# Involution on one core: one tap moves from VectorE to GpSimd, its weight copies go to ScalarE, and some steps change their tick

## The chip, the cores and the metric

The kernel runs on 1 core of one Trainium2 chip. The metric is the device time of one execution in microseconds (us). The core has five engines that work side by side and meet at semaphores: TensorE (PE in the profile), VectorE (DVE), ScalarE (ACT), GpSimd (POOL) and SyncE (SP, which issues most transfers). SBUF is the working memory, PSUM (eight banks, the tensor `ps`) the memory that TensorE writes and GpSimd doesn't reach.

## The reference

Layer 0 is an involution with a residual, layer 1 attention and a routed feed-forward block. Only layer 0 is touched. For each pixel it computes 49 weights (7 x 7 taps) per channel group, takes a softmax over them, and sums 49 shifted, weighted copies of the image:

```python
def _L0_conv_ref(x, ...):            # x: 4 x 256 x 56 x 56, group-normalized
    x1, x2, x3 = conv1x1(x, w1, b1), conv1x1(x, w2, b2), conv1x1(x, w3, b3)   # 32, 32 and 256 channels
    p = conv1x1(position(h, w, x.dtype), wp, bp)
    sub2 = x1[:, :, None] - unfold_patches(x2)      # 49 taps, reflect padding 3
    subp = p[:, :, None] - unfold_patches(p)
    y = relu(bn_eval(concatenate([sub2, subp]), ...))
    y = relu(bn_eval(conv1x1(y, cw1), ...))
    wgt = softmax(conv1x1(y, cw2, cb2), axis=2)     # over the 49 taps
    out = 0
    for idx in range(49):                           # i, j = idx // 7, idx % 7
        patch = x3p[:, :, i:i + h, j:j + w].reshape(n, 32, 8, h, w)
        out = out + patch * wgt[:, :, idx][:, :, None]
    return out
```

## The kernel before

**Bands.** After a first stage of projections the image is worked off in 14 bands of 4 rows (`RW`, `NW`); the 128 partitions hold 4 images x 32 groups. Two bands are always under way: band `b` is summed, while the weights of the next one, `a`, are computed. One such step is a `slot(a, b)`; each engine has its own `slot`, and a loop runs six times over two slots, with one slot before it and one behind it (`slots`). The slot of the last band has no `a`.

**Ticks.** A slot has 20 ticks (`NPAIR_D`), counted by `u`. The order of the work on each engine is written out by hand: lists say at which tick a step is issued, and every engine takes its instructions in that order.

**Summing band b.** Taps 0 to 38 (`ND`) are VectorE's, two at a time, nineteen pairs and a twentieth with one tap; taps 39 to 48 (`OWN`, ten) are GpSimd's. For a pair `p`, ScalarE copies the weights to a PSUM bank (`weights`, L519) and once more beside the products, as the ninth row that becomes the denominator (`denominators`, L526). VectorE multiplies the 8 channels of the window by them (`pair`, L689) into one of two buffers. TensorE adds the buffer to four PSUM banks with an identity matrix (`add`, L847). For one of its taps, GpSimd multiplies (L319) and copies the weights beside it (L320), into one of two buffers `own_buf`; TensorE adds it, ticks 10 to 19 (`OWN_AT`). When all 49 are added (`acc_done`), VectorE takes the reciprocal of the denominator (L638) and multiplies (L642), `divide`, and TensorE may begin the next band. Row `i` of the exponentials holds taps 7i to 7i + 6; a tap waits for its row (`exped`).

**The weights of band a.** GpSimd subtracts, `z(a, i)` (L287), for each of seven tap rows. ScalarE applies a ReLU (`first`, L532, at ticks 0, 1, 3, 5, 7, 9, 11). Then a chain of 14 steps, one a tick from tick 1 (`CH_AT`): TensorE (L818, L823), ScalarE (`second`, L543), TensorE (L834), ScalarE (`third`, L550, which writes the logits `lg`). All use the same PSUM banks, so the next begins when the last is written. `z(a, 5)` waits for the matmuls of tick 8, `z(a, 6)` for those of tick 10. VectorE takes a running maximum over tap rows (`rowmax`, L655; `MAX_AT`: rows 1 and 2 ahead of pair 9, the others ahead of pairs 11, 13, 15, 17) and then folds it to one value per pixel (L662 to L670, `maxed`). GpSimd subtracts that from the logits row by row (`shift`, L298), row 0 after all but two of its taps and row 1 after them; ScalarE takes the exponential (`expo`, L506), row 0 at tick 18, rows 1 to 6 in the next slot at ticks 0, 2, 4, 6, 8, 10 (`EXP_NEXT`). GpSimd's whole order is `POOL_ORDER`.

Of the kernel before, what the change touches and what calls it, by code (L numbers as in the profile page):

```python
# [15 lines left out]
P = 128  # L16
# [11 lines left out]
RW = 4  # L28
# [16 lines left out]
OWN = 10  # L45
ND = TAPS - OWN
NPAIR_D = (ND + 1) // 2
NCH = 2 * K7
# [6 lines left out]
MAX_AT = [CH_AT[2 * max(i, 2) + 1] + 3 for i in range(K7)]  # L55
FOLD_AT = MAX_AT[-1]
EXP_NOW_AT = FOLD_AT + 1
EXP_NEXT = {0: 1, 2: 2, 4: 3, 6: 4, 8: 5, 10: 6}
# [3 lines left out]
OWN_AT = [NPAIR_D - OWN + k for k in range(OWN)]  # L62
# [60 lines left out]
def conv_stage(nc, planes, x2_dram, a1_dram, pf_dram, cw1_bd, cw2_bd, ident_dram, conv_dram, keep):  # L123
    ctx = ExitStack()
    with ctx:
# [150 lines left out]
        def _(pool):  # L276
# [12 lines left out]
            def shift(b, i):  # L289
                pool.wait_ge(maxed, b.n + 1)  # L290
                if not b.early(1):
                    pool.wait_ge(den_in, NPAIR_D * (b.n - 1) + FREE_ROW_PAIRS if i < FREE_ROW else NPAIR_D * b.n)
                if i == FREE_ROW and not b.early(1):
                    pool.wait_ge(own_ready, 2 * OWN * b.n)
                if b.early(1) and i in (1, 4):
                    pool.wait_ge(planes_out[i % 2], 16 * NSTORE[i % 2])
                m = mx[:].rearrange("p (h w) -> p h w", w=W).unsqueeze(2).broadcast_to([P, RW, K7, W])
                pool.tensor_tensor(ex[:, i], lg[:, i], m, ALU.subtract).then_inc(shifted, 1)  # L298

            def own(b, k):  # L300
                t = ND + k
                i, j = t // K7, t % K7
                if k == 0:
                    pool.wait_ge(win_in[b.par], 16 * (b.half + 1))
                    if b.early(1):
                        pool.wait_ge(proj_done, NUNIT)
                if k == 1 and b.early(1):
                    pool.wait_ge(a1_out, 16 * NBK)
                pool.wait_ge(exped, b.q(i) + 1)
                if k == 0 and not b.early(1):  # L310
                    pool.wait_ge(acc_done, b.n)
                if k == 1 and not b.early(1):
                    pool.wait_ge(stored, 16 * RW * b.n)
                if k >= 2:
                    pool.wait_ge(own_used, (OWN - 1) * b.n + k - 1)
                w = ex[:, i, :, j, :]
                xw = win[b.par][:, i:i + RW, 0:SHARE, j:j + W]
                o = own_buf[k % 2]
                pool.tensor_tensor(o[:, :, 0:SHARE], w.unsqueeze(2).broadcast_to([P, RW, SHARE, W]), xw, ALU.mult).then_inc(own_ready, 1)  # L319
                pool.tensor_copy(o[:, :, SHARE], w).then_inc(own_ready, 1)  # L320
# [182 lines left out]
        def _(act):  # L503
# [10 lines left out]
            def weights(b, p):  # L514
                n = min(2, ND - 2 * p)
                act.wait_ge(exped, b.q((2 * p + n - 1) // K7) + 1)
                if not (b.early(1) and p < 2):
                    act.wait_ge(prod_ready, NPAIR_D * b.n + p - 1)
                act.activation(ps[:, 2 + p % 2, 0:n * PW].rearrange("p (n h w) -> p n h w", h=RW, w=W), tap_pair(p),  # L519
                               ACT.Copy).then_inc(w_out, 1)  # L520

            def denominators(b, p):
# [3 lines left out]
                act.activation(prod[p % 2][:, 0:n, :, SHARE], tap_pair(p), ACT.Copy).then_inc(den_in, 1)  # L526
# [28 lines left out]
            def slot(a, b):  # L555
                first, second, third = chain(a, b)
                for u in range(NPAIR_D if b else 0):
# [4 lines left out]
                    if a and b and u == EXP_NOW_AT:  # L562
                        expo(a, 0)
                    if b and u + 1 < NPAIR_D:
# [69 lines left out]
        def _(v):  # L634
# [39 lines left out]
            def slot(a, b):  # L674
                rowmax, fold = maxima(a, b)

                def pair(p):
# [6 lines left out]
                    w = ps[:, 2 + p % 2, 0:n * PW].rearrange("p (n h w) -> p n h w", h=RW, w=W).unsqueeze(3).broadcast_to([P, n, RW, SHARE, W])  # L684
# [3 lines left out]
                    o = prod[p % 2][:, 0:n, :, 0:SHARE]  # L688
# [105 lines left out]
        def _(pe):  # L794
# [44 lines left out]
            def slot(a, b):  # L839
# [11 lines left out]
                def pair(p, k):  # L851
                    if k == 0:
                        pe.wait_ge(den_in, NPAIR_D * b.n + p + 1)
                        await_ge(prod_ready, NPAIR_D * b.n + p + 1)
                    mm = add(prod[p % 2][:, k], p == 0 and k == 0, False)
# [3 lines left out]
                def own(k):  # L859
                    await_ge(own_ready, 2 * (OWN * b.n + k + 1))  # L860
# [6 lines left out]
                for u in range(NPAIR_D):  # L867
# [6 lines left out]
                    if b:  # L874
                        if 2 * u + 1 < ND:
                            pair(u, 1)
                        for k in range(OWN):
                            if OWN_AT[k] == u:
# [1880 lines left out]
```

## Time and profile before

| | us |
|---|---|
| median of 3 runs | 3521.96 (3514.76 to 3528.95) |
| the profiled execution | 3520.25 |
| its span | 3518.4 |
| busy: TensorE, VectorE, ScalarE, GpSimd | 3016.6, 2481.0, 1981.1, 2145.4 |

The profile is of one execution. Times in it count from the start of its span. It names the engine, the line of the kernel, the tiles written and read, and for an engine that stood idle what ended the wait. Of the span, the fourteen bands take the stretch from about 185 to 1631 us; the other stages follow. "Band 7" below is the slot whose first reciprocal starts at 926.86 (it closes the band before).

### The profile page before, as it was taken

To read this page: it belongs to the slowest core of one execution; us is meant where nothing else is said; L and a number is where in the kernel's file an instruction comes from. 1 tells how busy PE (TensorE), PEld (TensorE's weight loads), DVE (VectorE), ACT (ScalarE), POOL (GpSimd) and SP (SyncE) were. 2 spreads that over 40 slices of the span, in tenths; PEclk is the share of its full clock that TensorE was granted. 3 is DMA by queue.
4 is the path that set the end of the run, shared out by engine and by line. 5 is a ranking of instruction groups with operands and counts; after the bars stand their busy time and mean duration, and the time that the engine had idled before them with its cause. 6 is when DMAs were issued, how large, how long until landed. Compare 5 with 4: busy or idle time off the path is not lost. (4 is left out here: it accounts for less than half of the span.)

```text
span 3518.4 us, 102494 instructions
## 1 busy us (share of the span) xinstructions
PE 3016.6 (86%) x42638; PEld 1526.2 (43%) x42638; DVE 2481.0 (71%) x2173; ACT 1981.1 (56%) x3387; POOL 2145.4 (61%) x1235
## 2 busy tenths in 40 slices
PE   4988888888888887875899999999999989689997
PEld 1234434444444443432552354335334533267775
DVE  6369999999999999997763676476558655364322
ACT  1566556666655666642458656865775576434221
POOL 3369988889999888975671177037505751234433
PEclk9999899988999998988899999999999999799998
DMA  6531111221212122103011211111111122235544
GB/s 227 159 122 59 58 52 36 65 62 55 63 50 62 36 65 60 57 16 105 13 54 36 67 29 42 46 54 29 54 54 33 30 57 75 105 114 174 161 146 146
DMA packets 190699, 257.34 MB, mean 73 GB/s; under 512 B 88974, under 2 KB 151674, under 8 KB 188216
## 3 DMA queue, kind: packets, MB, share of 16 engines
q1 hardware_dynamic: 178348, 218.25, 20.6%
q0 software_dynamic: 11520, 32.55, 3.0%
q8 instruction: 357, 5.85, 0.7%
q14 instruction: 78, 0.64, 0.1%
q10 hardware_dynamic: 396, 0.05, 0.0%
HBM read 152.23 MB, written 79.27 MB: 66 GB/s over the span
## 5 line engine op out<-in xcount | busy, mean ns | idle before, releaser
L847 PE MATMUL ps<-late,ident 32*32 32x504 f32 x21952 | 1097.2, 645 | 213.8 <-issue 143.9
L689 DVE TENSOR_TENSOR late<-ps,late 128x3584 f32<-128x3584 f32 x280 | 1056.4, 3792 | 103.4 <-PE ps L847 95.0
L847 PEld LDWEIGHTS ps<-late,ident 32*32 32x32 f32 x21952 | 485.0, 108 | 471.7 <-issue 402.0
L319 POOL TENSOR_TENSOR late<-ex,late 128x1792 f32<-128x1792 f32 x140 | 530.0, 3786 | 64.0 <-PE ps L847 31.2
L1583 POOL TENSOR_TENSOR pool<-share 128x768 f32<-128x768 f32 (+1 forms) x200 | 348.3, 1748 | 182.8 <-ACT share L1779 135.7
L1825 ACT ACTIVATE phq<-ps 128x896 f32<-128x896 f32 x448 | 391.9, 920 | 72.8 <-PE ps L2177 68.7
L287 POOL TENSOR_TENSOR y<-xa 128x1568 f32<-128x1568 f32 x98 | 324.2, 3316 | 116.8 <-PE ps L823 115.8
L298 POOL TENSOR_TENSOR ex<-lg,mx 128x1568 f32<-128x1568 f32 x98 | 345.7, 3546 | 12.7 <-DVE mx L670 12.7
L2177 PE MATMUL ps<-qst,sel 96*128 96x448 bf16 x1120 | 296.3, 357 | 22.2 <-ACT phq L1825 16.4
L519 ACT ACTIVATE ps<-ex 128x448 f32<-128x448 f32 x280 | 149.4, 534 | 284.8 <-DVE late L689 284.7
L1928 DVE TENSOR_TENSOR pool<-ps,share 128x1280 f32<-128x1280 f32 (+1 forms) x200 | 295.5, 1481 | 4.0 <-ACT ps L1785 2.8
L2150 PE MATMUL ps<-pool,share 128*32 128x288 f32 (+3 forms) x3200 | 236.8, 412 | 27.5 <-ACT pool L1790 12.7
L543 ACT ACTIVATE y<-ps,u2c,s2c 128x784 f32<-128x784 f32 x189 | 189.3, 1001 | 126.0 <-PE ps L823 125.7
L818 PE MATMUL ps<-y,cw1bd 32*32 32x392 f32 x3136 | 217.1, 518 | 20.8 <-ACT y L532 9.6
L2127 PE MATMUL ps<-share,xt 128*128 128x256 f32 (+1 forms) x800 | 225.1, 406 | 6.5 <-ACT share L1786 5.5
L2177 PEld LDWEIGHTS ps<-qst,sel 96*128 96x128 bf16 x1120 | 82.8, 98 | 320.2 <-ACT phq L1825 172.8
L550 ACT ACTIVATE lg<-ps,par 128x784 f32<-128x784 f32 x196 | 179.1, 914 | 75.4 <-PE ps L834 75.2
L2046 DVE TENSOR_TENSOR at<-ps,rd 128x448 f32<-128x448 f32 x56 | 35.0, 624 | 260.1 <-PE ps L2242 238.1
L1008 POOL TENSOR_TENSOR lm20a<-t 128x448 f32<-128x448 f32 x16 | 18.2, 1138 | 325.4 <-DVE t L1880 325.4
L834 PE MATMUL ps<-y,cw2bd 32*32 32x392 f32 x3024 | 186.5, 523 | 28.1 <-ACT y L543 23.1
L655 DVE TENSOR_TENSOR run<-lg,run 128x1568 f32<-128x1568 f32 x70 | 195.6, 2794 | 2.2 <-issue 1.6
L2599 PE MATMUL ps<-xct,w_s 128*128 128x392 f32 x512 | 181.0, 499 | 11.2 <-DMA w_s<-in_w 6.8
(280 smaller groups left out, 5029.0 us busy)
## 6 DMA issues: line engine op xcount, KB each, us to landing
late<-planes SPq DMA_DIRECT2D x14, 2480.0 KB, 9.0
pf<-pf_dram SPq DMA_DIRECT2D x392, 55.1 KB
planes<-ex SPq DMA_DIRECT2D x7, 1984.0 KB, 9.4
conv_dram<-late SPq DMA_DIRECT2D x56, 224.0 KB, 4.8
t<-in_x SPq DMA_DIRECT2D x28, 448.0 KB, 4.0
xt<-conv_dram SPq DMA_DIRECT2D x28, 448.0 KB, 6.3
t_dram<-tout SPq DMA_DIRECT2D x28, 448.0 KB, 2.9
pool<-t_dram SPq DMA_DIRECT2D x24, 512.0 KB
```

What stands on the lines that cost most here:

```text
L287: pool.tensor_tensor(o, x1, x2, ALU.subtract).then_inc(z_ready, 1)
L298: pool.tensor_tensor(ex[:, i], lg[:, i], m, ALU.subtract).then_inc(shifted, 1)
L319: pool.tensor_tensor(o[:, :, 0:SHARE], w.unsqueeze(2).broadcast_to([P, RW, SHARE, W]), xw, ALU.mult).then_inc(own_ready, 1)
L689: v.tensor_tensor(o, w, xw, ALU.mult).then_inc(prod_ready, 1)
L818: pe.matmul(ps[at:at + 32, k + r // 2, 0:CW].rearrange("p (j w) -> p j w", w=W), diag(cw1, r), y[32 * r:32 * r + 32, :, h * W:(h + 1) * W] ...
L847: mm = pe.matmul(ps[32 * h:32 * h + 32, 4 + r, 0:DENC], diag(ident, r), x[32 * r:32 * r + 32, h].rearrange("p s w -> p (s w)"), start=begi ...
L1583: pool.tensor_tensor(phk[j % 2][0:r, :, ROT_V * DH:FLIN].rearrange("p h (r i) -> p h r i", i=DH), ki.unsqueeze(2).broadcast_to([r, HPG, RO ...
L1825: act.activation(dst, src, ACT.Square).then_inc(phq_done, 1)
L1928: v.tensor_tensor(phk[j % 2][0:r, :, DH:ROT_V * DH].rearrange("p h (r i) -> p h r i", i=DH), same.unsqueeze(2).broadcast_to([r, HPG, ROT_V ...
L2127: mm = pe.matmul(ps[0:r, 4 + j % 2, 0:HPG * DH + P], xn[:, k, j * P:j * P + r], wkv_s[:, k, hg, :], start=(k == 0), stop=(k == CH - 1))
L2150: pe.matmul(ps[DH * h:DH * h + DH, f, 0:hi - lo], kv[j % 3][0:r, v0:v0 + DH], phk[j % 2][0:r, h, lo:hi], start=(j == 0), stop=(j == NT - 1))
L2177: mm = pe.matmul(ps[:, h, 0:CT], sel[:, f, :], qst[:, h, ch(c)], start=True, stop=True)
```

## The change

GpSimd takes 11 taps (38 to 48) and VectorE 38, which is 19 full pairs; a slot now has 19 ticks. GpSimd's taps are added at ticks 9 to 18, the last two of them both at tick 18. GpSimd no longer copies weights: ScalarE does (`own_denominators`), one tick ahead of the tap's addition and before the denominators of the next pair. It counts them in `den_in`, so that TensorE waits for both. A copy waits for its row's exponential and, from the third on, for the buffer that TensorE has to be done with (`own_used`). The exponentials of rows 1 to 6 go at ticks 0, 2, 4, 9, 7, 10: row 5 ahead of row 4; `EXP_TURN` gives the place of a row in that order. The maxima of rows 1 and 2 stand ahead of pair 8. Since the number of pairs is odd, the buffers and PSUM banks of pairs alternate from band to band.

```diff
@@ -42,9 +42,10 @@
     args[-1]["project"] = args[:-1]
 
 
-OWN = 10
+OWN = 11
 ND = TAPS - OWN
 NPAIR_D = (ND + 1) // 2
+NDEN = NPAIR_D + OWN
 NCH = 2 * K7
 CW = K7 * W
 DENC = (SHARE + 1) * W
@@ -52,14 +53,15 @@
 FREE_ROW = 2
 FREE_ROW_PAIRS = (FREE_ROW * K7 + 1) // 2
 CH_AT = [1 + c for c in range(NCH)]
-MAX_AT = [CH_AT[2 * max(i, 2) + 1] + 3 for i in range(K7)]
+MAX_AT = [CH_AT[5] + 2] * 3 + [CH_AT[2 * i + 1] + 3 for i in range(3, K7)]
 FOLD_AT = MAX_AT[-1]
 EXP_NOW_AT = FOLD_AT + 1
-EXP_NEXT = {0: 1, 2: 2, 4: 3, 6: 4, 8: 5, 10: 6}
+EXP_NEXT = {0: 1, 2: 2, 4: 3, 7: 5, 9: 4, 10: 6}
+EXP_TURN = [0] + [list(EXP_NEXT.values()).index(i) + 1 for i in range(1, K7)]
 FIRST_AT = [0] + [2 * i - 1 for i in range(1, K7)]
 POOL_ORDER = [("z", 0), ("z", 1), ("shift", 2), ("shift", 3), ("z", 2), ("shift", 4), ("shift", 5), ("z", 3), ("shift", 6),
               ("z", 4), ("z", 5), ("own", 0), ("own", 1), ("z", 6)] + [("own", k) for k in range(2, OWN - 2)]
-OWN_AT = [NPAIR_D - OWN + k for k in range(OWN)]
+OWN_AT = [NPAIR_D - OWN + 1 + k for k in range(OWN)]
 SCALE_AT = 1
 NMAX = K7 + 2
 
@@ -289,9 +291,9 @@
             def shift(b, i):
                 pool.wait_ge(maxed, b.n + 1)
                 if not b.early(1):
-                    pool.wait_ge(den_in, NPAIR_D * (b.n - 1) + FREE_ROW_PAIRS if i < FREE_ROW else NPAIR_D * b.n)
+                    pool.wait_ge(den_in, NDEN * (b.n - 1) + FREE_ROW_PAIRS if i < FREE_ROW else NDEN * b.n)
                 if i == FREE_ROW and not b.early(1):
-                    pool.wait_ge(own_ready, 2 * OWN * b.n)
+                    pool.wait_ge(own_ready, OWN * b.n)
                 if b.early(1) and i in (1, 4):
                     pool.wait_ge(planes_out[i % 2], 16 * NSTORE[i % 2])
                 m = mx[:].rearrange("p (h w) -> p h w", w=W).unsqueeze(2).broadcast_to([P, RW, K7, W])
@@ -306,7 +308,7 @@
                         pool.wait_ge(proj_done, NUNIT)
                 if k == 1 and b.early(1):
                     pool.wait_ge(a1_out, 16 * NBK)
-                pool.wait_ge(exped, b.q(i) + 1)
+                pool.wait_ge(exped, b.q(EXP_TURN[i]) + 1)
                 if k == 0 and not b.early(1):
                     pool.wait_ge(acc_done, b.n)
                 if k == 1 and not b.early(1):
@@ -317,7 +319,6 @@
                 xw = win[b.par][:, i:i + RW, 0:SHARE, j:j + W]
                 o = own_buf[k % 2]
                 pool.tensor_tensor(o[:, :, 0:SHARE], w.unsqueeze(2).broadcast_to([P, RW, SHARE, W]), xw, ALU.mult).then_inc(own_ready, 1)
-                pool.tensor_copy(o[:, :, SHARE], w).then_inc(own_ready, 1)
 
             def slot(a, b):
                 for kind, k in POOL_ORDER:
@@ -513,17 +514,33 @@
 
             def weights(b, p):
                 n = min(2, ND - 2 * p)
-                act.wait_ge(exped, b.q((2 * p + n - 1) // K7) + 1)
+                act.wait_ge(exped, b.q(max(EXP_TURN[t // K7] for t in range(2 * p, 2 * p + n))) + 1)
                 if not (b.early(1) and p < 2):
                     act.wait_ge(prod_ready, NPAIR_D * b.n + p - 1)
-                act.activation(ps[:, 2 + p % 2, 0:n * PW].rearrange("p (n h w) -> p n h w", h=RW, w=W), tap_pair(p),
+                act.activation(ps[:, 2 + (NPAIR_D * b.n + p) % 2, 0:n * PW].rearrange("p (n h w) -> p n h w", h=RW, w=W), tap_pair(p),
                                ACT.Copy).then_inc(w_out, 1)
 
             def denominators(b, p):
                 n = min(2, ND - 2 * p)
                 if not (b.early(1) and p < 2):
                     act.wait_ge(summed, NPAIR_D * b.n + p - 1)
-                act.activation(prod[p % 2][:, 0:n, :, SHARE], tap_pair(p), ACT.Copy).then_inc(den_in, 1)
+                act.activation(prod[(NPAIR_D * b.n + p) % 2][:, 0:n, :, SHARE], tap_pair(p), ACT.Copy).then_inc(den_in, 1)
+
+            def own_denominators(b, k):
+                t = ND + k
+                i, j = t // K7, t % K7
+                act.wait_ge(exped, b.q(EXP_TURN[i]) + 1)
+                if k == 0 and b.early(1):
+                    act.wait_ge(proj_done, NUNIT)
+                if k == 1 and b.early(1):
+                    act.wait_ge(a1_out, 16 * NBK)
+                if k == 0 and not b.early(1):
+                    act.wait_ge(acc_done, b.n)
+                if k == 1 and not b.early(1):
+                    act.wait_ge(stored, 16 * RW * b.n)
+                if k >= 2:
+                    act.wait_ge(own_used, (OWN - 1) * b.n + k - 1)
+                act.activation(own_buf[k % 2][:, :, SHARE], ex[:, i, :, j, :], ACT.Copy).then_inc(den_in, 1)
 
             def chain(a, b):
                 def first(i):
@@ -561,6 +578,8 @@
                         weights(b, u + 2)
                     if a and b and u == EXP_NOW_AT:
                         expo(a, 0)
+                    if b and u + 1 in OWN_AT:
+                        own_denominators(b, OWN_AT.index(u + 1))
                     if b and u + 1 < NPAIR_D:
                         denominators(b, u + 1)
                     if a and u in CH_AT:
@@ -681,11 +700,11 @@
                     v.wait_ge(w_out, NPAIR_D * b.n + p + 1)
                     if not (b.early(1) and p < 2):
                         v.wait_ge(summed, NPAIR_D * b.n + p - 1)
-                    w = ps[:, 2 + p % 2, 0:n * PW].rearrange("p (n h w) -> p n h w", h=RW, w=W).unsqueeze(3).broadcast_to([P, n, RW, SHARE, W])
+                    w = ps[:, 2 + (NPAIR_D * b.n + p) % 2, 0:n * PW].rearrange("p (n h w) -> p n h w", h=RW, w=W).unsqueeze(3).broadcast_to([P, n, RW, SHARE, W])
                     at = [t // K7 * SHARE * WP + t % K7 for t in range(2 * p, 2 * p + n)]
                     x = win[b.par][:]
                     xw = bass.AP(x.tensor, x.offset + at[0], [x.ap[0], [at[-1] - at[0], n], [SHARE * WP, RW], [WP, SHARE], [1, W]])
-                    o = prod[p % 2][:, 0:n, :, 0:SHARE]
+                    o = prod[(NPAIR_D * b.n + p) % 2][:, 0:n, :, 0:SHARE]
                     v.tensor_tensor(o, w, xw, ALU.mult).then_inc(prod_ready, 1)
 
                 for u in range(NPAIR_D):
@@ -850,14 +869,15 @@
 
                 def pair(p, k):
                     if k == 0:
-                        pe.wait_ge(den_in, NPAIR_D * b.n + p + 1)
+                        pe.wait_ge(den_in, NDEN * b.n + p + 1 + sum(t <= p for t in OWN_AT))
                         await_ge(prod_ready, NPAIR_D * b.n + p + 1)
-                    mm = add(prod[p % 2][:, k], p == 0 and k == 0, False)
+                    mm = add(prod[(NPAIR_D * b.n + p) % 2][:, k], p == 0 and k == 0, False)
                     if 2 * p + k == min(2 * p + 1, ND - 1):
                         mm.then_inc(summed, 1)
 
                 def own(k):
-                    await_ge(own_ready, 2 * (OWN * b.n + k + 1))
+                    pe.wait_ge(den_in, NDEN * b.n + OWN_AT[k] + k + 1)
+                    await_ge(own_ready, OWN * b.n + k + 1)
                     mm = add(own_buf[k % 2], False, k == OWN - 1)
                     if k < OWN - 1:
                         mm.then_inc(own_used, 1)
@@ -875,7 +895,7 @@
                         if 2 * u + 1 < ND:
                             pair(u, 1)
                         for k in range(OWN):
-                            if OWN_AT[k] == u:
+                            if min(OWN_AT[k], NPAIR_D - 1) == u:
                                 own(k)
 
             pe.wait_ge(small_in, N_SMALL)
```

## Rows read from the trace of the kernel before

**Rows 1.** The page's groups: line, tiles, count, busy us, mean ns, idle before.

```profile
L689 DVE TENSOR_TENSOR late<-ps,late 128x3584 f32<-128x3584 f32 x280 | 1056.4, 3792 | 103.4 <-PE ps L847 95.0
```

**Rows 2.** Band 7: stretch, busy us of PE, PEld, DVE, ACT, POOL; granted clock.

```profile
926.90:1031.20 104.30, 86.80 (x2128) 43.66 (x2128) 95.94 (x33) 64.59 (x82) 93.08 (x35) 0.90 0.18 55
```

**Rows 3.** VectorE in time: start us, us, operation; first and thirteenth reciprocal.

```profile
305.72 1.56 DVE L638 RECIPROCAL run<-ps 128x224 f32<-128x224 f32 x1 [0.50 <-PE ps L847]
...
1548.01 1.56 DVE L638 RECIPROCAL run<-ps 128x224 f32<-128x224 f32 x1 [0.31 <-PE ps L847]
```

**Rows 4.** The same view of VectorE, band 7.

```profile
926.86 1.56 DVE L638 RECIPROCAL run<-ps 128x224 f32<-128x224 f32 x1 [0.42 <-PE ps L847]
...
963.35 3.89 DVE L689 TENSOR_TENSOR late<-ps,late 128x3584 f32<-128x3584 f32 x1 [0.45 <-PE ps L847]
...
968.97 4.79 DVE L655 TENSOR_TENSOR run<-lg,run 128x1568 f32<-128x1568 f32 x1
973.68 7.67 DVE L689 TENSOR_TENSOR late<-ps,late 128x3584 f32<-128x3584 f32 x2
...
1010.53 2.58 DVE L655 TENSOR_TENSOR run<-lg,run 128x1568 f32<-128x1568 f32 x1
...
1015.04 0.39 DVE L670 TENSOR_TENSOR mx<-ps,run 128x224 f32<-128x224 f32 x1
...
1023.46 2.02 DVE L689 TENSOR_TENSOR late<-ps,late 128x1792 f32<-128x1792 f32 x1 [0.43 <-PE ps L847]
1027.38 3.89 DVE L689 TENSOR_TENSOR late<-ps,late 128x3584 f32<-128x3584 f32 x1 [1.90 <-PE ps L847]
1031.18 1.55 DVE L638 RECIPROCAL run<-ps 128x224 f32<-128x224 f32 x1
```

**Rows 5.** Lines L655, L320, L526 in twelve bands: count, min/median/max ns.

```profile
L655 DVE TENSOR_TENSOR run<-lg,run x60: 1777/2582/4907, 345.9 to 1527.7; 128x1568 f32<-128x1568 f32 x60
...
L320 POOL COPY late<-ex x122: 359/374/1956, 299.9 to 1546.2; 128x224 f32<-128x224 f32 x122
...
L526 ACT ACTIVATE late<-ex x242: 390/566/581, 301.3 to 1548.3; 128x448 f32<-128x448 f32 x121
```

**Rows 6.** GpSimd in time, band 7.

```profile
960.10 3.28 POOL L287 TENSOR_TENSOR y<-xa 128x1568 f32<-128x1568 f32 x1 [0.42 <-PE ps L823]
968.85 3.26 POOL L287 TENSOR_TENSOR y<-xa 128x1568 f32<-128x1568 f32 x1 [5.47 <-PE ps L823]
973.37 3.94 POOL L319 TENSOR_TENSOR late<-ex,late 128x1792 f32<-128x1792 f32 x1 [1.26 <-ACT ex L506]
...
991.18 1.93 POOL L320 COPY late<-ex 128x224 f32<-128x224 f32 x1
...
1013.30 4.29 POOL L319 TENSOR_TENSOR late<-ex,late 128x1792 f32<-128x1792 f32 x1
...
1025.34 3.70 POOL L319 TENSOR_TENSOR late<-ex,late 128x1792 f32<-128x1792 f32 x1
```

**Rows 7.** TensorE in time, ticks 9, 11, 12 of band 7.

```profile
977.66 2.15 PE L847 MATMUL ps<-late,ident 32*32 32x504 f32 x32 [4.61 <-issue]
...
987.04 0.82 PE L818 MATMUL ps<-y,cw1bd 32*32 32x392 f32 x9
...
992.09 0.82 PE L818 MATMUL ps<-y,cw1bd 32*32 32x392 f32 x9
```

**Rows 8.** Two stretches of band 7, columns as in rows 2.

```profile
977.66:980.00 2.34, 2.34 (x45) 1.24 (x57) 2.34 (x1) 0.98 (x2) 2.34 (x1) 0.50 0.02 7
982.00:1002.20 20.20, 19.46 (x549) 11.78 (x547) 20.20 (x7) 15.45 (x19) 17.44 (x7) 1.00 0.15 47
```

**Rows 9.** ScalarE in time, band 7.

```profile
971.79 1.50 ACT L506 ACTIVATE ex<-ex 128x1568 f32<-128x1568 f32 x1
```

**Rows 10.** The last band in time: GpSimd's first tap, VectorE's last reciprocal.

```profile
1585.24 3.70 POOL L319 TENSOR_TENSOR late<-ex,late 128x1792 f32<-128x1792 f32 x1 [17.73 <-issue]
...
1627.13 1.56 DVE L638 RECIPROCAL run<-ps 128x224 f32<-128x224 f32 x1 [4.65 <-PE ps L847]
```

## The prediction

> **What bounds the kernel now.** I read five views in this order. First the page's groups: one line of VectorE, the product of a pair of taps (L689), is 1056 us, and its idle time in front is 95 us, all of it for TensorE [rows 1]. Then the stretches by band: in a band of 104.3 us VectorE is busy 95.9, GpSimd 93.1, TensorE 86.8 and ScalarE 64.6 [rows 2]. Two engines are nearly full, so neither can be relieved alone. Then the reciprocals that close a band: from the first to the thirteenth there are twelve bands in 1242.3 us, 103.5 us each [rows 3]. The change touches only this stretch and what lies at its ends, up to 1631 us; the 1887 us behind it stay as they are.
>
> Last I followed band 7 on VectorE, GpSimd, ScalarE and TensorE, from the reciprocal at 926.86 to the next at 1031.18 [rows 4]. Up to tick 8 the ticks come every 4.34 us, set by the serial chain of the next band (matmul, ReLU, matmul, bias) with ScalarE full; VectorE's pair takes only 3.80 of it. At tick 9 two maxima are put in front of pair 9. The second takes 4.79 us where the shortest takes 1.78 [rows 4, 5], because GpSimd's subtraction that began at 968.85 runs until 972.1 [rows 6]: the maximum (two SBUF inputs) and a GpSimd operation don't run side by side. It works both ways: the copy at 991.18 took 1.93 us, the median copy 0.37 [rows 5, 6]. TensorE stands for 4.61 us for pair 9 and then runs at a granted clock of 0.50, that is 1.2 GHz [rows 7, 8]. From there to tick 14 a tick costs TensorE 5.05 us, since it has one tap of GpSimd more [rows 7]. At the end the last GpSimd tap begins at 1025.34 and is ready at about 1029.4 with its copy [rows 6]; TensorE adds it (1.15 us) and the reciprocal runs at 1031.18. VectorE's pair 0 of the next band ends at 1031.27 [rows 4], so both paths end within 0.7 us. A gain needs both.
>
> **The change part by part.**
>
> VectorE loses pair 19, which had one tap: 2.02 us, 1.93 in steps from start to start, and the 0.43 us of waiting before it [rows 4].
>
> GpSimd gets an eleventh product (3.71 us, 3.65 in steps) and loses ten copies. An undisturbed copy costs 0.37, ten of them 3.7 [rows 5, 6]. So its busy time doesn't change. The stretched part of a copy, 1.6 us, isn't saved: it is the time in which a maximum holds the port, and the next product will wait for it instead. So GpSimd gains nothing by work, only by an earlier start.
>
> ScalarE takes eleven copies of 224 columns. Its own copy of that size, the lone tap's denominator, takes 0.39 us [rows 5]: 11 x 0.39 = 4.3 us, less some 0.8 for the two copies of that width that vanish with pair 19. That is +3.5 us on 64.6 of 104. They stand at ticks 8 to 18; only 8, 9 and 10 are tight. Every copy from the third on waits until TensorE has used the buffer, with the denominators of the next pair queued behind it and TensorE waiting for those; TensorE has passed that buffer in the tick before, so I take 0. Its other end is 1.15 us a band, at the last tick, where the next band's first weights stand behind the eleventh copy, which waits for GpSimd's ninth tap to be added. It costs nothing as long as GpSimd's end is later, which it is in my walk.
>
> Row 5's exponential goes from tick 8 to tick 7, row 4's to tick 9, both beside a ReLU of 1.5 us. In front of the first tap GpSimd was idle 1.26 us for the exponential that began at 971.79 [rows 6, 9]. A tick of 4.34 us sooner it begins at about 967.5 and is done at 969.0, before GpSimd's subtraction ends at 972.1. So tap 0 starts at 972.1 and not 973.37: 1.27 us gained. The doubled tick 7 delays ScalarE's ReLU of tick 8 by 1.5 us, hidden behind pair 8 (below); that of tick 9 costs the chain 0.7 us, taken into the walk.
>
> Maxima 1 and 2 go in front of pair 8, at about 962.8 instead of 967.2. Row 2's logits are written by then. GpSimd's subtraction at 960.10 ends at 963.4 [rows 6], so the first waits 0.6, the second meets an idle GpSimd: VectorE is through at 967.0. Pair 8 then runs 967.0 to 970.9 (before 963.35) and pair 9 starts at 970.8 (before 973.68) [rows 4]: 2.9 us gained. TensorE's stall of 4.61 us becomes one of about 2.2 (from 968.8 to 971.0). Whether its clock then falls no row shows: the stop of 4.61 us was followed by 0.50, the stretch with hardly a gap ran at 1.00 [rows 7, 8]. 2.2 lies between; I take no fall, since the stop is less than half of the one that shows it; the other end is 2.3 us at half clock, some 1.2 us lost per band.
>
> GpSimd's taps are now used from tick 9 on, so six ticks and not five cost 5.05 us, starting at 974.2.
>
> The walk on from 972.1 on GpSimd (its eleven taps are 0 to 10): taps 0 and 1 to 979.5; maximum 3 takes the port to 981.3; the seventh subtraction (3.26) to 984.6; taps 2 and 3 to 992.0; maximum 4, come at 988.8, waits 3.2 us for that and holds it to 993.8; taps 4 and 5 to 1001.2; tap 6 waits for TensorE, behind maximum 5, to 1003.2 and runs to 1006.9; tap 7 to 1010.9; maximum 6 to 1012.6. VectorE writes the band's maximum at about 1014.4 (before 1015.04 [rows 4]). Tap 8 takes 4.3 like the one at 1013.30 [rows 6], to 1016.9; then subtraction of row 0 (3.5) to 1020.4, taps 9 and 10 to 1027.7; TensorE 1.15 and the handover to 1029.05. Before: 1031.18. VectorE comes free at about 1028.5. So the band is **2.1 us** shorter, with GpSimd as the path that ends last. The start of the following band hangs on GpSimd's last tap as well (its next subtractions feed the chain), and moves by the same.
>
> For thirteen bands that is 27.3 us. The last band has no maxima and no chain: its tap 0 began at 1585.24 and the reciprocal came 4.65 us after VectorE was done [rows 10]. With the exponential 3.8 us sooner, no copies and 11 x 3.65 us, GpSimd's taps would be ready at 1622; then TensorE is late, with pair 18 and two taps behind it: 1620.6 + 2.3 + 2.3 = 1625.2, 1.8 us sooner. The sum is 29 us. The profiled execution took 3520.25 us (span 3518.4, 1.85 around it), 1.7 below the median of 3521.96: **3491 us**.
>
> Bounds: without any port wait of maxima 3 to 6 GpSimd would come 2 to 3 us sooner per band (4.5 us x 13 = 59, 3462); with the half clock at tick 8, the 1.15 of the copies and 0.8 more of port waits the band's gain is minus 1.0 (3533).
>
> **The port, by row and by rule.** The 4.79 us and the 1.93 us above are what the trace shows [rows 4, 6]. The Trainium skill (SBUF — State Buffer, section on the two separate sides) says of the pair that VectorE and GpSimd share that it is an exclusive lock held for the whole instruction, and that the loser blocks fully. By that rule a maximum that comes just after a GpSimd product has begun waits for all of it; the trace agrees as far as 3.0 us of wait. This speaks against the change, and gives the second rival.
>
> **Rivals.**
>
> *The gain is given back at TensorE and ScalarE.* TensorE falls to half clock at tick 8, the chain ticks stay at 5.05, ScalarE is late after ticks 7 and 9. For it: TensorE was busy 19.46 of 20.20 us from 982 to 1002, so it has little to give there, and the stop of 4.61 us was followed by the low clock [rows 8]. Against it: the stop gets shorter. Gain 0.5 us per band, 7 in all: 3513. Decides if pair 10 starts later than 976.
>
> *Slower: the maxima collide with products.* GpSimd had idle time before its products and short copies between them, and the maxima waited about 0.8 (2.58 - 1.78, the one at 1010.53 [rows 4]). With products back to back each of the four maxima may wait up to 3.7. VectorE has to its credit 1.93 + 2.4 + 0.45 + 0.43 + 1.90 = 7.1 us per band (pair, second maximum, the waits of tick 8 and before the last two pairs [rows 4]); it is slower than before once the four waits come to over 3.2 + 7.1 = 10.3 us, 2.6 each. My walk has 4.1. At 3.4 each: +3.3 us per band, 13 bands: 3563.
>
> *More than forecast.* Products and maxima fall into step with waits below 1 us and TensorE stays at 2.4 GHz: 3.5 to 4.5 us per band, about 3466.
>
> *It doesn't do what it says:* if the exponential of row 5 at tick 7 still ends after 972.1, GpSimd starts as late as before, and the gain is 0.8 us per band: 3508. I count it with the first rival.
>
> **How the numbers follow.** Forecast (1.3 to 3.5 us per band, 3471 to 3502): 0.50. Gain given back (3502 to 3537): 0.26. More: 0.12. Slower: 0.12. What a measurement can tell from no change is 0.5%, 17.6 us. Faster is forecast and more, 0.62; same 0.26; slower 0.12. The range leaves out the slower case and a part of the larger one: 3462 to 3536.
>
> **What would show it.** In the changed profile: 19 pairs of one form per band, no GpSimd copy, eleven products; maxima 1 and 2 in 0.5 to 1 us of wait in all; GpSimd without idle for the exponential before tap 0; TensorE's stop at tick 8 about 2 us; reciprocals every 101.4 us; the wait before the reciprocal pointing at GpSimd's last tap. Wrong if the maxima of rows 3 to 6 last over 4 us on average, if the granted clock at tick 8 is 0.50, or if ScalarE's copies wait for TensorE.

## The result and the profile after

The changed kernel takes 3529.82 us (median of 20 runs) where the kernel before takes 3517.05: the ratio is 1.0038, 95% interval 1.003 to 1.0045. It is slower by 13 us; 29 us faster was forecast. Its profiled execution took 3529.81 us, with a span of 3528.0, 9.6 more than before. Up to the last reciprocal the profile of the changed kernel is 15.1 us longer; the stages behind it, which the change doesn't touch, came out 5.5 us shorter in this execution (1885.8 against 1891.3).

The groups of the page (line, tiles, count; busy us, mean ns; idle time before), answering to [rows 1]:

```profile
L708 DVE TENSOR_TENSOR late<-ps,late 128x3584 f32<-128x3584 f32 x266 | 1026.9, 3885 | 112.8 <-PE ps L866 70.0
...
L321 POOL TENSOR_TENSOR late<-ex,late 128x1792 f32<-128x1792 f32 x154 | 623.1, 4066 | 57.8 <-PE ps L866 43.0
```

VectorE's pairs are 266 of one form (14 x 19) and take 29.5 us less than before, as they should. Its idle time went from 103.4 to 112.8 us. GpSimd's product of a tap has a mean of 4066 ns; before it was 3786. The work was moved as meant, the waits grew.

Reciprocals on VectorE, the first and the thirteenth, answering to [rows 3]:

```profile
306.32 1.56 DVE L657 RECIPROCAL run<-ps 128x224 f32<-128x224 f32 x1 [0.30 <-PE ps L866]
...
1564.57 1.56 DVE L657 RECIPROCAL run<-ps 128x224 f32<-128x224 f32 x1 [0.39 <-PE ps L866]
```

Twelve bands in 1258.2 us are 104.85 us each, 1.33 more than the 103.52 before: 16 us over twelve bands. The first reciprocal came 0.6 us later, and the last band got shorter (77.6 us against 79.1), close to the 1.8 us forecast.

Busy time in stretches (us of PE, PEld, DVE, ACT, POOL, then the granted clock): band 7, answering to [rows 2], and two short stretches used below.

```profile
936.66:1039.99 103.33, 82.72 (x2128) 41.25 (x2128) 96.51 (x31) 67.03 (x92) 92.37 (x26) 0.93 0.19 56
454.20:458.00 3.80, 3.80 (x69) 2.12 (x80) 3.62 (x1) 1.46 (x4) 3.80 (x2) 0.50 0.07 27
979.80:983.60 3.80, 3.79 (x107) 1.85 (x112) 3.80 (x2) 2.12 (x4) 3.80 (x2) 1.00 0.15 52
```

In band 7 ScalarE is busy 67.0 us (64.6 before: 2.4 more, 3.5 were forecast) and GpSimd 92.4 (93.1, no change forecast). So the costs of the instructions were right, or on the safe side. Band 7 is one of the three shortest after the change; the mean of a band tells more than this one.

**Where the time sits.** The end of a band before the change, in time, GpSimd and VectorE:

```profile
1010.53 2.58 DVE L655 TENSOR_TENSOR run<-lg,run 128x1568 f32<-128x1568 f32 x1
...
1011.40 1.93 POOL L320 COPY late<-ex 128x224 f32<-128x224 f32 x1
...
1013.14 0.92 DVE L662 TENSOR_TENSOR ps<-run 128x672 f32<-128x672 f32 x1
1013.30 4.29 POOL L319 TENSOR_TENSOR late<-ex,late 128x1792 f32<-128x1792 f32 x1
```

The sixth maximum (L655) holds the port that VectorE and GpSimd share until about 1013.1. GpSimd's copy of tap 6's weights, asked for at 1011.40, waits for it and is done at 1013.33. The fold's first step (L662, two SBUF inputs as well) begins at 1013.14 and takes 0.92 us. GpSimd's next product waits for the fold, 4.29 instead of 3.72.

The same place after the change, VectorE, then GpSimd:

```profile
1018.60 1.78 DVE L674 TENSOR_TENSOR run<-lg,run 128x1568 f32<-128x1568 f32 x1
1020.41 4.22 DVE L681 TENSOR_TENSOR ps<-run 128x672 f32<-128x672 f32 x1
...
1025.61 0.39 DVE L689 TENSOR_TENSOR mx<-ps,run 128x224 f32<-128x224 f32 x1
...
1018.62 5.29 POOL L321 TENSOR_TENSOR late<-ex,late 128x1792 f32<-128x1792 f32 x1
1026.16 3.50 POOL L300 TENSOR_TENSOR ex<-lg,mx 128x1568 f32<-128x1568 f32 x1 [2.25 <-DVE mx L689]
```

Between the end of the sixth maximum and the start of the fold (L681) VectorE's rows show 0.03 us. GpSimd's product 8 has been asking since 1018.62, so it goes in between, whole: it ends at 1023.91, and the fold takes 4.22 us instead of 0.92. This happens in every band but the first, whose fold has no taps of GpSimd beside it; the line's own view (count: min/median/max ns), before and after:

```profile
L662 DVE TENSOR_TENSOR ps<-run x14: 856/915/916, 175.1 to 1530.3; 128x672 f32<-128x672 f32 x14
...
L681 DVE TENSOR_TENSOR ps<-run x14: 858/4229/4244, 178.0 to 1544.1; 128x672 f32<-128x672 f32 x14
```

### The profile page after: what moved, and what is told of

The parts are those of the page before. It is cut to its first block and busy times, and to the rows that moved or that the text cites. A ratio compares the mean times of both kernels' runs of the same rounds, so it can differ in the third digit from the quotient of the medians.

```text
span 3528.0 us, 102962 instructions
## 1 busy us (share of the span) xinstructions
PE 2995.9 (85%) x42638; PEld 1510.8 (43%) x42638; DVE 2481.4 (70%) x2159; ACT 2009.9 (57%) x3513; POOL 2138.5 (61%) x1109
## 5 line engine op out<-in xcount | busy, mean ns | idle before, releaser
L866 PE MATMUL ps<-late,ident 32*32 32x504 f32 x21952 | 1056.5, 634 | 239.3 <-DVE late L708 142.9
L708 DVE TENSOR_TENSOR late<-ps,late 128x3584 f32<-128x3584 f32 x266 | 1026.9, 3885 | 112.8 <-PE ps L866 70.0
L866 PEld LDWEIGHTS ps<-late,ident 32*32 32x32 f32 x21952 | 455.8, 107 | 520.0 <-issue 449.9
L321 POOL TENSOR_TENSOR late<-ex,late 128x1792 f32<-128x1792 f32 x154 | 623.1, 4066 | 57.8 <-PE ps L866 43.0
L507 ACT ACTIVATE ex<-ex 128x1568 f32<-128x1568 f32 x98 | 147.4, 1504 | 107.9 <-POOL ex L300 107.9
```

The source lines that it names most:

```text
L708: v.tensor_tensor(o, w, xw, ALU.mult).then_inc(prod_ready, 1)
L866: mm = pe.matmul(ps[32 * h:32 * h + 32, 4 + r, 0:DENC], diag(ident, r), x[32 * r:32 * r + 32, h].rearrange("p s w -> p (s w)"), start=begi ...
```

## The experiments

Each kernel ran on the same chip beside the kernel before: e1 to e4 on one chip, e5 to e8 on a second, e9 to e12 on a third. On these the kernel before takes 3491 to 3494 us, not 3517, so kernels are compared by their ratios and by the length of a band, the mean from the first to the thirteenth reciprocal. Behind the last reciprocal the profiles of the experiments are some 20 us shorter than the two of the result (1864 to 1868 us against 1886 and 1891), which is most of that difference and lies outside the bands. A band's length is from one profiled execution of each kernel; that of e12 took 3480 us where the median of its ten runs is 3490, the others lie within about 5 us of theirs. "Fold" is the median of its first step.

| kernel | fold, us | band, us | ratio to before (95% interval) |
|---|---|---|---|
| before | 0.92 | 103.52 | 1 |
| changed | 4.23 | 104.85 | 1.0038 (1.003 to 1.0045) |
| e1_shift_early | 0.87 | 103.49 | 0.999 (0.998 to 1.000) |
| e2_max_back | 4.2 | 106.07 | 1.0109 (1.0088 to 1.013) |
| e3_row4_first | 4.2 | 104.61 | 1.004 (1.0025 to 1.0056) |
| e4_copies_only | 4.22 | 104.83 | 1.006 (1.0036 to 1.0084) |
| e5_keep_copy7 | 0.92 | 101.47 | 0.9934 (0.9913 to 0.9956) |
| e6_copies_shift | 0.87 | 103.07 | 0.998 (0.9968 to 0.9991) |
| e7_max_split | 4.2 | 105.63 | 1.0095 (1.0079 to 1.0112) |
| e8_before_max8 | 0.92 | 103.60 | 1.0025 (1.001 to 1.0039) |
| e9_keep_copy5 | 4.23 | 104.60 | 1.0053 (1.0036 to 1.007) |
| e10_keep_all | 0.92, twice 4.2 | 104.36 | 1.0037 (1.0019 to 1.0055) |
| e11_ten_keep6 | 0.92 | 101.98 | 0.9953 (0.9936 to 0.9969) |
| e12_keep7_maxback | 0.92 | 102.65 | 0.9994 (0.998 to 1.0007) |

My theory after the result was the port: the loss is the fold's wait for a GpSimd product. The rivals were TensorE's clock (a longer stop before pair 17, a new one at tick 8) and ScalarE (copies in the way of the chain and of the next band's first weights).

**e1_shift_early.** No product between the sixth maximum and the fold.

```diff
-              ("z", 4), ("z", 5), ("own", 0), ("own", 1), ("z", 6)] + [("own", k) for k in range(2, OWN - 2)]
+              ("z", 4), ("z", 5), ("own", 0), ("own", 1), ("z", 6)] + [("own", k) for k in range(2, OWN - 3)]
...
                 if a:
                     shift(a, 0)
                 if b:
+                    own(b, OWN - 3)
                     own(b, OWN - 2)
```

> The changed kernel with one edit: GpSimd subtracts row 0 for the next band one tap earlier, ahead of its last three taps instead of its last two. So no GpSimd product stands between the sixth maximum and the fold. Port theory (the fold's first step waits 3.3 us for that product, 4.22 where it took 0.92): the fold's first step falls back to 0.92, the band's maximum is written 3.3 us sooner, three taps instead of two follow it, so a band gets 2.0 to 2.6 us shorter: ratio to the kernel before near 0.996, about 3501 us. TensorE-clock theory (the stop of 7.8 us in front of pair 17 is the cost): the stop falls to 4.5 us and the half clock stays; gain under 0.5 us per band, ratio 1.002. ScalarE theory (next band's first weights wait behind the eleventh copy): the copy waits for a tap that is now later by one product, so no gain or a loss, ratio 1.004 to 1.008.

The fold went to 0.87 us, and the ratio from 1.0038 to 0.999. The band lost 1.4 us, less than the 2.0 to 2.6 expected: the maximum is written 3.4 us sooner, but GpSimd now has three taps after it and ends the band 17 us after it instead of 15. ScalarE's theory, which wanted no gain, falls, and so does the clock's, which allowed under 0.5 us per band: the stop before pair 17 went from 7.8 to 4.4 us as it said, but the gain is nearly three times that.

**e2_max_back and e3_row4_first.** One part of the change undone each.

```diff
-MAX_AT = [CH_AT[5] + 2] * 3 + [CH_AT[2 * i + 1] + 3 for i in range(3, K7)]
+MAX_AT = [CH_AT[2 * max(i, 2) + 1] + 3 for i in range(K7)]
```

> The changed kernel with the first two maxima back in front of pair 9. Port theory: the second meets GpSimd's subtraction again (4.7 us), but the first no longer meets the one before; the stop of TensorE moves back to tick 9. If the move was a gain (as forecast, 2.9 us less of waiting), the band gets 1 to 2 us longer, ratio 1.008. If the move was a loss (TensorE at half clock at tick 8 in the bands where it stops for 4 us, maxima and GpSimd products out of step afterwards), it gets shorter by up to 1.5 us, ratio 1.000.

```diff
-EXP_NEXT = {0: 1, 2: 2, 4: 3, 7: 5, 9: 4, 10: 6}
+EXP_NEXT = {0: 1, 2: 2, 4: 3, 6: 4, 7: 5, 10: 6}
```

> The changed kernel with row 4's exponential at tick 6 as before and row 5's at tick 7, so tick 9 has only the ReLU. ScalarE theory: the chain at tick 10 comes 0.7 us sooner (TensorE's wait of 0.85 us there goes), up to 0.7 us per band, ratio 1.001. Port and clock theories: the maxima and the last taps set the band, so no difference, ratio 1.004.

With the maxima back the kernel is 0.7% slower still (1.0109): their move was a gain, 1.2 us per band. Row 4's exponential makes no difference that can be measured (1.004).

**e4_copies_only.** The kernel before with ScalarE's copies, ten taps; as an edit of the changed kernel:

```diff
-OWN = 11
+OWN = 10
...
-MAX_AT = [CH_AT[5] + 2] * 3 + [CH_AT[2 * i + 1] + 3 for i in range(3, K7)]
+MAX_AT = [CH_AT[2 * max(i, 2) + 1] + 3 for i in range(K7)]
...
-EXP_NEXT = {0: 1, 2: 2, 4: 3, 7: 5, 9: 4, 10: 6}
+EXP_NEXT = {0: 1, 2: 2, 4: 3, 6: 4, 8: 5, 10: 6}
...
-OWN_AT = [NPAIR_D - OWN + 1 + k for k in range(OWN)]
+OWN_AT = [NPAIR_D - OWN + k for k in range(OWN)]
```

> The kernel before with one part of the change alone: ScalarE copies the weights of GpSimd's ten taps, everything else as before. Port theory: GpSimd loses ten copies of 0.37 us, its products follow each other directly and meet the maxima and the fold; what the copies gave back is lost in waits: ratio 0.999 to 1.004. ScalarE theory: the copies delay the denominators and the next band's first weights: ratio over 1.003. Forecast of the prediction (GpSimd's end sets the band): each band 1 to 3 us shorter, ratio 0.990 to 0.996.

```profile
L681 DVE TENSOR_TENSOR ps<-run x14: 858/4220/4231, 178.1 to 1546.7; 128x672 f32<-128x672 f32 x14
```

The copies alone cost 0.6%, and the fold's first step is at 4.22 us in this kernel too. GpSimd does 0.37 us less ten times a band and the kernel gets slower. By the number alone this fits ScalarE's theory (over 1.003) and not mine (0.999 to 1.004); e6 and e11 below leave the same copies on ScalarE and decide between the two.

**e5_keep_copy7.** GpSimd makes one copy of eleven again, the one between products 7 and 8.

```diff
+KEEP = (7,)
-NDEN = NPAIR_D + OWN
+NDEN = NPAIR_D + OWN - len(KEEP)
...
                 pool.tensor_tensor(o[:, :, 0:SHARE], w.unsqueeze(2)..., xw, ALU.mult).then_inc(own_ready, 1)
+                if k in KEEP:
+                    pool.tensor_copy(o[:, :, SHARE], w).then_inc(own_ready, 1)
...
-                    if b and u + 1 in OWN_AT:
+                    if b and u + 1 in OWN_AT and OWN_AT.index(u + 1) not in KEEP:
```

> The changed kernel, but GpSimd makes one of its eleven copies itself again: that of tap 7, which comes between the products 7 and 8, where VectorE's sixth maximum and the fold follow each other. GpSimd gets 0.37 us more work and ScalarE 0.38 less. Port theory: at the end of the sixth maximum the turn passes to whoever waits; now it is a copy of 0.37 us and not a product of 3.7, so the fold's first step takes 0.9 to 1.3 us instead of 4.22, the band's maximum comes 2.9 to 3.3 us sooner, and after it GpSimd has product 8, row 0's subtraction and two products to do: band 0 to 1.5 us shorter, ratio 0.998 to 1.003. If the fold's 3.3 us have another cause (the work of GpSimd, not its order), the fold stays at 4.2 and the ratio at 1.004 or above.

VectorE and GpSimd at the same place, here of the eighth band, and the fold's line:

```profile
1094.67 1.77 DVE L683 TENSOR_TENSOR run<-lg,run 128x1568 f32<-128x1568 f32 x1
1096.47 0.92 DVE L690 TENSOR_TENSOR ps<-run 128x672 f32<-128x672 f32 x1
...
1091.00 3.73 POOL L328 TENSOR_TENSOR late<-ex,late 128x1792 f32<-128x1792 f32 x1 [0.29 <-PE ps L875]
1094.67 2.00 POOL L330 COPY late<-ex 128x224 f32<-128x224 f32 x1
1096.64 4.30 POOL L328 TENSOR_TENSOR late<-ex,late 128x1792 f32<-128x1792 f32 x1
```

```profile
L690 DVE TENSOR_TENSOR ps<-run x14: 856/918/919, 174.9 to 1502.0; 128x672 f32<-128x672 f32 x14
```

The copy asks at 1094.67 (2.00 us with its wait), takes the turn after the sixth maximum, and the fold starts at 1096.47 and takes 0.92. The ratio is 0.9934: faster than both kernels, by more than either theory had expected. Against the changed kernel the band is 3.38 us shorter, the 3.3 of the fold. I had expected GpSimd's work behind the maximum to eat most of it. It didn't, since GpSimd had been waiting there too: 2.25 us for the maximum and 1.50 for its buffer in the rows of the changed kernel above and below, nothing at either place in this band.

**e9_keep_copy5.** The control: the same edit, the same work at another place.

```diff
-KEEP = (7,)
+KEEP = (5,)
```

> Control for the kept copy: GpSimd again makes one of its eleven copies, the same 0.37 us of work, but that of tap 5, which doesn't come between the sixth maximum and the fold. Port theory (the turn at that one place decides): the fold's first step stays at 4.2 us and the ratio at about 1.004, as in the changed kernel. If the gain of the kept copy of tap 7 came from its work, from ScalarE's relief or from another shift of GpSimd's phase, this one gains as well: ratio 0.993 to 0.998.

```profile
L690 DVE TENSOR_TENSOR ps<-run x14: 858/4228/4245, 177.3 to 1540.4; 128x672 f32<-128x672 f32 x14
```

No gain, 1.0053. So it is neither the work nor ScalarE's relief, but the place of the copy.

**e6_copies_shift and e11_ten_keep6.** Two ways of taking the fold's wait out of e4_copies_only: row 0's subtraction one tap earlier, as in e1, and the copy of tap 6 kept, ahead of the product that slips in with ten taps. As edits of e4_copies_only, in part; first e6, then e11:

```diff
+                    own(b, OWN - 3)
                     own(b, OWN - 2)
```

```diff
+KEEP = (6,)
```

> ScalarE copies the weights of ten taps, all else as before, and GpSimd subtracts row 0 one tap earlier, so that no product stands in front of the fold. Port theory: the 3.3 us of the fold, which the copies alone had caused, go; three taps instead of two follow the maximum: band 1 to 2 us shorter than with the copies alone, ratio 0.996 to 1.000. ScalarE theory: the copies themselves cost, the ratio stays at 1.004 to 1.008.

> The copies alone (ten taps, everything else as before), with GpSimd making tap 6's copy itself, which with ten taps is the one in front of the product that slipped ahead of the fold. Port theory: the fold's first step goes from 4.2 to about 0.9 us, the band gets 1 to 3 us shorter than with the copies alone (ratio 1.006), ratio 0.990 to 0.999. What is left between this and the eleven-tap kernel with one kept copy (0.993) is what the eleventh tap, the maxima and the exponentials bring. ScalarE theory: no change, 1.004 to 1.008.

```profile
L690 DVE TENSOR_TENSOR ps<-run x14: 858/916/916, 174.6 to 1509.6; 128x672 f32<-128x672 f32 x14
```

From 1.006 to 0.998 and to 0.9953; the fold's line shown is that of e11. With ScalarE's copies in place the loss goes with the fold's wait, so ScalarE's theory falls here as well. The copies are worth moving, all but one.

**e10_keep_all.** The eleventh tap, the maxima and the exponentials as changed, no copy moved. As an edit of e5_keep_copy7:

```diff
-KEEP = (7,)
+KEEP = tuple(range(OWN))
```

> The changed kernel with all eleven copies back on GpSimd: eleventh tap, maxima and exponentials as changed. Port theory: the fold's first step is 0.92, but GpSimd has ten copies of 0.37 more than with one kept, 3.7 us of work on the engine that ends the band, less what of it lies in waits: 1 to 3.5 us per band longer than with tap 7's copy alone, ratio 0.997 to 1.006. If moving the copies to ScalarE brought nothing but the lost turn, the ratio is that of the single kept copy, 0.993.

```profile
L690 DVE TENSOR_TENSOR ps<-run x14: 856/916/4232, 178.0 to 1542.6; 128x672 f32<-128x672 f32 x14
```

1.0037, and in two of thirteen bands the product got in all the same (the maximum of 4232 ns). An eleventh tap without the relief of the copies makes GpSimd the slower engine: the reciprocals wait 2.7 to 4.1 us for its last tap, where they wait 0.3 to 0.4 in the changed kernel.

**e8_before_max8 and e12_keep7_maxback.** The move of the maxima alone, in the kernel before; and undone in e5_keep_copy7.

```diff
-MAX_AT = [CH_AT[2 * max(i, 2) + 1] + 3 for i in range(K7)]
+MAX_AT = [CH_AT[5] + 2] * 3 + [CH_AT[2 * i + 1] + 3 for i in range(3, K7)]
```

> The kernel before with one part of the change alone: the first two maxima in front of pair 8. The copies keep their place on GpSimd, pairs and taps are as before. Prediction's theory: the second maximum no longer waits 3.0 us, 0.6 to 1.5 of it comes back on the first: band 1 to 2 us shorter, ratio 0.993 to 0.996. Clock theory: TensorE falls to half clock at tick 8 as it did at tick 9, no loss by it, but ticks 9 to 14 are then bound by TensorE: ratio 0.997 to 1.001.

> The changed kernel with tap 7's copy kept on GpSimd and the first two maxima back in front of pair 9. With the fold's wait gone, this shows what the move of the maxima brings: by the comparison with the fold's wait in place it was 0.7%, so ratio 1.000; if that 0.7% depended on the fold, the ratio is between 0.993 and 0.997.

Alone the move brings nothing: the ratio is 1.0025 where the prediction's theory had 0.993 to 0.996 and the clock's 0.997 to 1.001. Its profile doesn't show that loss in the bands, which are as long as before (103.60 and 103.52 us), so what the 0.25% are stays open. In these bands the third maximum starts 1.2 us sooner than before, and the fourth takes 5.27 us on average (2.45 before): what the first two save goes there. With the copies moved and the turn kept the same move is worth 0.6% (0.9994 against 0.9934), by the bands 1.2 us each, as much as with the fold's wait in place.

**e7_max_split.** The changed kernel with the second maximum back at tick 9, the first at tick 8.

```diff
-MAX_AT = [CH_AT[5] + 2] * 3 + [CH_AT[2 * i + 1] + 3 for i in range(3, K7)]
+MAX_AT = [CH_AT[5] + 2] * 2 + [CH_AT[5] + 3] + [CH_AT[2 * i + 1] + 3 for i in range(3, K7)]
```

> The changed kernel with the first maximum in front of pair 8 and the second in front of pair 9, so that TensorE stops twice for about 2 us and not once for up to 4. Clock theory: no stretch at 0.50 at ticks 8 and 9 in any band, pair 10 starts in time everywhere, and the nine bands in which it was 1.2 to 2.0 us late gain that: band 0.9 to 1.4 us shorter on average, ratio 1.000. Port theory: the second maximum meets the subtraction of tick 8 or GpSimd's first product and waits 2 to 3 us more, so nothing or a loss, ratio 1.004 to 1.010.

1.0095: the second maximum waits again (1.77 to 4.68 us, 3.13 on average against 1.79). VectorE's wait for TensorE before pair 10, 1.0 us per band in the changed kernel, is gone. So splitting TensorE's stop costs more at the port than it gives back. It doesn't show that the clock costs nothing, since both moved, and the low clock stayed in part: in band 2 the second of the two stops was 3.11 us, and 0.50 followed.

## Why the prediction was wrong, step by step

**The step that failed** is in the walk: "maximum 6 to 1012.6. VectorE writes the band's maximum at about 1014.4". It gives the fold no wait at all. I had priced the turn at the port for the maxima, in the walk and in the second rival, and not for the fold, whose first step reads two SBUF inputs as well. The next sentence, "Tap 8 takes 4.3 like the one at 1013.30", puts the fold ahead of the product; that order was read off a row in front of which the copy had taken the turn, and the change removes this copy. And the sentence that "the stretched part of a copy ... isn't saved" looked at the copy's time and not at what it did: it took the turn between two VectorE instructions that follow each other at 0.03 us. With the copy gone a product of 3.5 us takes that turn. That is 3.3 us per band, thirteen times 43 us. The forecast was 29 us faster, the result 13 slower: the difference is 42. By the band: 3.3 us more for the fold, 2.0 less for all the rest, together the 1.33 more; 2.1 less was forecast. e5_keep_copy7, the changed kernel without that wait, has a band of 101.47 us; the forecast was 101.4.

That the rest comes out so well is in part luck. Against the kernel before, the walk has the band's maximum 0.6 us sooner and the stretch from it to the reciprocal 1.5 us shorter; in e5 it is 1.2 and 0.85. The parts were off by more than the sum, as the next paragraphs show.

A second piece of luck: 3530 lies inside the stated range of 3462 to 3536, and among the times given to the first rival (3502 to 3537). That rival was to decide itself by pair 10 starting later than 976, 49.1 us after the reciprocal; pair 10 starts 47.6 us after it on average and at most 48.6. The low clock it spoke of is there (below), but it took 1.0 us per band and not the gain.

**The near rival.** "Slower: the maxima collide with products" had the right kind of mechanism, and the wrong instruction and point of decision. VectorE in band 7, from pair 7 to the fourth maximum:

```profile
967.55 3.89 DVE L708 TENSOR_TENSOR late<-ps,late 128x3584 f32<-128x3584 f32 x1 [0.45 <-PE ps L866]
971.36 2.60 DVE L674 TENSOR_TENSOR run<-lg 128x1568 f32<-128x1568 f32 x1
974.00 1.79 DVE L674 TENSOR_TENSOR run<-lg,run 128x1568 f32<-128x1568 f32 x1
975.71 11.48 DVE L708 TENSOR_TENSOR late<-ps,late 128x3584 f32<-128x3584 f32 x3
...
997.18 4.60 DVE L674 TENSOR_TENSOR run<-lg,run 128x1568 f32<-128x1568 f32 x1
```

Maxima 3 to 6 last 2.12, 4.56, 1.78 and 1.79 us on average, so their waits come to 3.1 us per band; the walk had 4.1 and the rival needed 10.3. Maximum 4 waits 2.8 us (forecast 3.2), and 5 and 6 nothing. Why those two come just as GpSimd is between products, no run takes apart.

**The first two maxima.** The second meets no GpSimd work any more: 1.79 us against 4.51 on average before, as forecast. The first waits 1.45 us on average (3.23 us long), not 0.6; in band 7 it was 0.8. The wait did no harm: it is long where the maximum comes early, and pair 8 starts 39.0 to 39.2 us after the reciprocal in every band, sooner than the 40.1 of the walk. The move is a gain all the same (e2_max_back, e12_keep7_maxback).

**TensorE's clock at tick 8.** I took no fall for a stop of 2.2 us. TensorE's first matmuls after the stop, band 2 and band 7:

```profile
454.17 1.85 PE L866 MATMUL ps<-late,ident 32*32 32x504 f32 x17 [3.99 <-DVE late L708]
...
979.74 1.14 PE L866 MATMUL ps<-late,ident 32*32 32x504 f32 x32 [2.43 <-DVE late L708]
```

In band 2 the stop was 3.99 us and the next 3.8 us ran at 0.50, 1.2 GHz; in band 7 it was 2.43 and they ran at 1.00 (the two short stretches in the windows above). Where the stop was near the 2.2 us of the walk the assumption mostly held: of five stops of 1.8 to 2.5 us, four were followed by 1.00 and one, of 2.14 us, by 0.65. But in the other seven bands the stop was 2.9 to 4.0 us, since the first maximum waited longer. What it costs is VectorE's wait for TensorE before pair 10: nothing in bands 3, 7, 9 and 11, 1.6 to 1.9 us in bands 2, 6, 8 and 12, where the clock was at 0.50, and 0.8 to 1.0 in the other four, at 0.61 to 0.65. That is 1.0 us per band on average, near the bound of 1.2 that I had put on it; it is read from the trace, no run took it away by itself.

**The end of the band.** The forecast had GpSimd's last two products back to back, and ScalarE's last copy costing nothing. TensorE, ScalarE, GpSimd and VectorE there:

```profile
1029.94 2.00 PE L866 MATMUL ps<-late,ident 32*32 32x504 f32 x32 [7.77 <-DVE late L708]
...
1034.79 0.39 ACT L543 ACTIVATE late<-ex 128x224 f32<-128x224 f32 x1 [3.59 <-PE ps L866]
...
1034.83 3.71 POOL L321 TENSOR_TENSOR late<-ex,late 128x1792 f32<-128x1792 f32 x1 [1.50 <-PE ps L866]
...
1035.74 3.89 DVE L708 TENSOR_TENSOR late<-ps,late 128x3584 f32<-128x3584 f32 x1 [2.14 <-ACT ps L520]
1039.99 1.56 DVE L657 RECIPROCAL run<-ps 128x224 f32<-128x224 f32 x1 [0.37 <-PE ps L866]
```

TensorE stands for 7.77 us, for the sixth maximum, the fold and pair 17, then begins to add pair 17 at half clock (0.53 from 1026 to 1030, 0.50 in the 2 us from 1029.94). GpSimd's last product and ScalarE's eleventh copy wait for it, until 1034.8, and VectorE's next pair 0 waits for the weights behind that copy: 2.0 to 3.5 us in each of thirteen bands, 34.5 in all. Even so the reciprocal waits 0.37 us for the last tap, and from the band's maximum to the reciprocal it is 14.9 us on average, against 15.9 before; 14.65 was forecast. So the copy costs nothing beside GpSimd's tap, which ends later, as the prediction said.

**The signs.** Of the three signs of being wrong two came, the granted clock of 0.50 at tick 8 (in four bands) and ScalarE's copies waiting for TensorE; neither is the step that failed. The maxima of rows 3 to 6 last 2.57 us on average, not over 4. The fold's first step was not among them.

**What was right:** the costs of each instruction, the earlier first tap (1.8 us sooner on average, forecast 1.3), the last band (1.5 us shorter, forecast 1.8), ScalarE's small load. Row 4's exponential at tick 9 was to cost the chain 0.7 us; with it back at tick 6 (e3) the band is 0.24 us shorter, which the ratio doesn't show.

**What stays open.** Maxima at tick 9 beside eleven taps and one copy kept (e12) give 0.9994, the ten-tap kernel with one copy kept (e11) 0.9953. So the eleventh tap with its exponentials costs some 0.4% there (by the spans of their profiles 0.3%). With the earlier maxima it reaches 0.9934, and whether that is better than 0.9953 the intervals leave open, since they overlap. Why, I have not taken apart.

## What to carry to other kernels

VectorE and GpSimd took turns at their port instruction by instruction. Before a short instruction is taken off one of two such engines, look at which of its instructions will be waiting in its place, and whether the other engine has two instructions close together there (here a maximum and a fold) that the short one kept together; here an instruction of 0.37 us was worth 3.3. Where an experiment shows the parts of a change not adding up (e8 no gain, e12 against e5 a gain of the same part), test each part in the surroundings in which it is meant to stay.

## What the runs showed of the hardware

A gap of 0.03 us between two VectorE instructions with two SBUF inputs was enough for a waiting GpSimd product to go first and hold the port for 3.5 us, in 13 bands of 13. The Trainium skill (SBUF — State Buffer, section on the two separate sides) says that the one who starts first holds the shared pair for the whole instruction; the trace agrees, and shows beside it that a waiting GpSimd instruction starts first there. VectorE's products (one input in PSUM, one in SBUF) ran beside GpSimd's without any stretch: 3.89 us at the start and at the end.
